# Two attention blocks on one core: MLP kept in rows, group norm per image, residual rows on GpSimd, one product of query and key weights

## The chip, the cores and the metric

One core of one Trainium2 chip. The metric is the device time of one execution in microseconds (us). Engine names: PE is TensorE (matrix products and transposes), DVE is VectorE, ACT is ScalarE, POOL is GpSimd, SP issues the DMAs. Each engine works through its own list of instructions in order; between engines the program waits on semaphores that are written out by hand.

## What is computed

The input x is 4 images of 16x16 pixels and 128 channels, all in float32. Layer 0 is a deformable attention with 8 heads, followed by an MLP; layer 1 is a group norm and a full attention inside each image. Cut to what the change touches:

```python
# layer 0, after q, the offsets and the 64 sampled keys of each image
attn = softmax(einsum(qh, kh)); msa = att @ mo_w + mo_b
z = msa + x
out0 = gelu(layernorm(z, ln_g, ln_b) @ mlp_w + mlp_b) + z
# layer 1, on v = out0
xg = group_norm(v, 32 groups of 4 channels over an image) * gn_gamma + gn_beta
q = (xg @ wq + bq) / sqrt(128); k = xg @ wk + bk; val = xg @ wv + bv
out = softmax(q @ k.T) @ val @ wo + bo + v
```

## The kernel before

The channels are 128, so one image is two tiles of 128 pixels (T = 8 tiles, B = 4 images). "Rows" means pixels on the partitions and channels along the free dimension; "transposed" means channels on the partitions and the 256 pixels of an image along it.

The program is one `build` function (line 69) in which each engine's list is written out: helper functions for each step, then a long sequence of calls. Nothing is scheduled by a compiler. The steps that matter here are these.

- Loads (lines 266 to 275) and normalisation of x, a convolution as 256 small products on PE, the offsets, the sampling weights `bilin` and the sampled keys. This fills the first 23 us.
- First attention, tile by tile (0 to 7): PE makes the scores of all heads (`score_tile`), DVE takes their maximum (`max_tile`, line 684) and subtracts it (`shift_tile`, line 691), PE transposes (`transpose_scores`, line 1099), ACT takes the exponential (`exp_tile`, line 451), PE multiplies with the values and with ones (`value_tile`), ACT inverts the sum by a logarithm and an exponential (lines 458, 465), DVE scales (`norm_tile`, line 700), PE projects (`out_project`), DVE adds the residual (`z_tile`, line 705). There is one set of four PSUM banks for the scores, so `score_tile(i)` waits for `shift_tile(i - 1)`.
- Norm of z and MLP, image by image: statistics on DVE, `z_scale` on POOL (a power of -0.5, line 334), `z_offset` on DVE (line 726), z_hat on ACT or DVE, two transposes (z and z_hat) on PE, the MLP in transposed form with `mlp_wg`, GELU on ACT, the sum `x1_t` on DVE (line 732). PE then transposes x1 back (`x1_transpose`, line 1168) and DVE adds the output bias to it (`x1_residual`, line 737): that is the residual in rows for the end.
- Group norm in two sets of two images: `gn_stats`, `gn_aggr` on DVE (lines 742, 746), `gn_apart` on PE (means of a group), `gn_square` and `gn_mean` on DVE (lines 752, 758), `gn_spread` on PE, `gn_var` on DVE (line 763), `gn_pow` on POOL (line 340), `norm_image` on DVE (line 769). The gamma is folded into three weights on POOL (`weights_scale`).
- Second attention, image by image: products q, k and v on PE (`project_q`, `project_k`, `project_v`), copied out by DVE (q, line 776) and ACT (k, line 495; v, line 489); scores (`score_image`), maximum on DVE (line 781), exponential on ACT (line 503), transposes of the probabilities p on PE (line 1250), copies (line 245), product with v, and `finish_tile` on DVE (lines 789, 791). SP sends y to memory.

A matmul of float32 stands as two records in the trace, a transpose as one. All matmuls but the transposes are recorded at the helper's line 917. The trace names a tensor without its digits, so `q1` is q, `k1` is k, `p1` is p and `v1` is v, and the PSUM banks 1 to 4 are called score.

## Time and profile before

| | us |
|---|---|
| median of 3 runs (lowest, highest) | 70.53 (70.19, 70.92) |
| the profiled execution, its own time | 71.08 |
| its span (first to last instruction) | 69.2 |
| PE busy in the span | 62.3 |
| DVE busy | 45.7 |
| ACT busy | 39.1 |
| POOL busy | 19.7 |

Times in the trace count from the start of the span. Neighbouring instructions of one engine overlap a little, since the next one is started before the last one has written out; so the distance of two starts (the pitch) is shorter than the duration of one, and both are used below. TensorE's granted clock was at its full 1.00 in every stretch.

### The profile page before, as it was taken

The numbers are of one execution on the slowest core, as the hardware profiler recorded it, in microseconds if no ns is written. First come the engines' busy times: TensorE is split into PE (matmuls) and PEld (weight loads), VectorE is DVE, ScalarE is ACT, GpSimd is POOL, SyncE is SP. The second block draws the span as 40 slices with busy tenths as digits, with TensorE's granted clock in tenths as the row PEclk, the third lists the DMA queues.
The fourth block names the chain that finished last, engine by engine and source line by source line (L and its number), as shares of the span: only waits on it lengthen the run. The fifth ranks groups of instructions, "written<-read, shape, count | busy, mean of one in ns | idle before, by whom it ended". The sixth has DMA issues, their size and how long they took to land.

```text
span 69.2 us, 2174 instructions
## 1 busy us (share of the span) xinstructions
PE 62.3 (90%) x822; PEld 47.5 (69%) x822; DVE 45.7 (66%) x154; ACT 39.1 (56%) x103; POOL 19.7 (28%) x31
## 2 busy tenths in 40 slices
PE   4999789988999998999979899998999999999940
PEld 1326379977587746786769778665578889998930
DVE  0258973102724598856999988699599894677570
ACT  5210349821920497758454799996272399849400
POOL 6002999994000001938004231321300300000000
PEclk9999999999999999999999999999999999999999
DMA  0779794000000000000000000000000000020212
GB/s 0 190 219 244 205 387 164 9 0 0 9 0 9 0 0 0 5 9 0 0 0 5 9 0 0 0 0 0 0 9 0 0 0 0 0 76 5 76 66 86
DMA packets 3051, 3.08 MB, mean 45 GB/s; under 512 B 225, under 2 KB 2657, under 8 KB 3042
## 3 DMA queue, kind: packets, MB, share of 16 engines
q1 hardware_dynamic: 3042, 2.96, 14.0%
q8 instruction: 6, 0.10, 0.6%
q14 instruction: 3, 0.02, 0.1%
HBM read 2.44 MB, written 0.52 MB: 43 GB/s over the span
## 4 chain that ended last, share of the span: by engine, by line
PE 57%; DVE 18%; issue 7%; DMA 6%; ACT 5%; SPq 2%; DVEq 0%; ACTq 0%
PE bank L917 30%; PE score L917 21%; DMA x_hw<-x 6%; DVE smax L684 4%; DVE s_sub L691 2%; PE bank L1099 2%; ACT p_t L451 2%; ACT log_sum L458 1%; DVE y L791 1%; SPq L267 1%; PE bank L1250 1%; PE score L1250 1%; DVE st L612 1%; DVE zst L709 1%; DVE q_conv L601 1%
## 5 line engine op out<-in xcount | busy, mean ns | idle before, releaser
L684 DVE TENSOR_REDUCE smax<-score 128x8 f32<-128x512 f32 x8 | 5.5, 690 | 1.6 <-PE score L917 1.4
L917 PE MATMUL bank<-q_ph,wd 128*32 128x84 f32 (+5 forms) x256 | 6.2, 249 | 0.0
L917 PEld LDWEIGHTS bank<-q_ph,wd 128*32 128x32 f32 x256 | 5.4, 110 | 1.1 <-ACT q_ph L382 0.8
L917 PE MATMUL score<-warm 128*128 128x512 bf16 x12 | 5.0, 569 | 1.0 <-POOL warm L289 1.0
L691 DVE TENSOR_TENSOR s_sub<-score,smax 128x512 f32<-128x512 f32 x8 | 5.5, 690 | 0.2
L318 POOL TENSOR_TENSOR x_res<-x_st,msa_bias 128x1024 f32<-128x1024 f32 x1 | 2.4, 2369 | 11.0 <-ACT msa_bias L423 11.0
L300 POOL TENSOR_TENSOR wd<-pack_early 128x512 f32<-128x512 f32 x4 | 4.1, 1046 | 4.9 <-DVE x_hat L624 4.9
L917 PE MATMUL score<-k_blk,qh 32*128 32x128 f32 x64 | 4.0, 319 | 1.2 <-DVE s_sub L691 1.1
L451 ACT ACTIVATE p_t<-bank 128x512 f32<-128x512 f32 x8 | 4.5, 592 | 0.9 <-PE bank L1099 0.9
L1099 PE MATMUL bank<-pack_early,s_sub 128*128 128x128 f32 x32 | 5.0, 285 | 0.0
L334 POOL TENSOR_TENSOR zrs<-zve,neg_half 128x2 f32<-128x2 f32 x4 | 2.8, 697 | 7.2 <-DVE zve L717 7.2
L917 PEld LDWEIGHTS score<-k_blk,qh 32*128 32x128 f32 x64 | 2.6, 182 | 2.9 <-issue 2.7
L612 DVE BATCH_NORM_STATS2 st<-x_hw 128x6 f32<-128x128 f32 x8 | 1.8, 283 | 3.7 <-DMA x_hw<-x 3.7
L503 ACT ACTIVATE p<-bank,nmax 128x256 f32<-128x256 f32 x8 | 3.5, 475 | 1.1 <-DVE nmax L781 1.0
L1099 PEld LDWEIGHTS bank<-pack_early,s_sub 128*128 128x128 f32 x32 | 3.4, 141 | 1.1 <-issue 0.4
L917 PE MATMUL bank<-k,q 128*128 128x256 f32 x16 | 3.9, 384 | 0.0
L634 DVE COPY q_ph<-score 128x256 f32<-128x256 f32 x2 | 0.8, 425 | 4.4 <-PE score L917 4.4
L917 PE MATMUL score<-q_conv,pack_early 128*32 128x128 f32 x64 | 2.5, 275 | 1.1 <-DVE q_conv L601 0.6
L917 PEld LDWEIGHTS score<-warm 128*128 128x128 bf16 x12 | 1.4, 130 | 3.1 <-issue 2.1
L495 ACT ACTIVATE k<-score,cols 128x256 f32<-128x256 f32 x4 | 1.9, 474 | 2.6 <-DVE q L776 2.6
L917 PE MATMUL bank<-p_t,v_blk 128*32 128x128 f32 x64 | 3.3, 280 | 0.0
L340 POOL TENSOR_TENSOR grs<-gve,neg_half 128x2 f32<-128x2 f32 x2 | 1.4, 690 | 6.7 <-DVE gve L763 6.7
(180 smaller groups left out, 161.6 us busy)
## 6 DMA issues: line engine op xcount, KB each, us to landing
x_st<-x SPq DMA_DIRECT2D x1, 512.0 KB, 6.8
pack_late<-late SPq DMA_DIRECT2D x1, 448.0 KB, 7.4
out<-y SPq DMA_DIRECT2D x3, 128.0 KB, 1.7
pack_fold<-fold SPq DMA_DIRECT2D x1, 320.0 KB, 4.7
pack_mid<-mid SPq DMA_DIRECT2D x1, 273.0 KB, 5.8
x_hw<-x SPq DMA_DIRECT2D x2, 128.0 KB, 2.4
x_hw<-x SPq DMA_DIRECT2D x1, 256.0 KB, 4.2
pack_early<-early SPq DMA_DIRECT2D x1, 184.0 KB, 2.7
```

What stands on the lines that cost most here:

```text
L300: pool.tensor_tensor(wd[:, n:n + WD_CHUNK].rearrange("p n k j -> p (n k) j"), w("ident32").unsqueeze(1).to_broadcast([P, WD_CHUNK * PHASES ...
L318: pool.tensor_tensor(x_res[:, :, :], x_st[:, :, :].rearrange("p b (s c) -> p (b s) c", s=S), msa_bias[:, :].unsqueeze(1).to_broadcast([P, ...
L334: pool.tensor_tensor(zrs[:, 2 * b:2 * b + 2], zve[:, 2 * b:2 * b + 2], neg_half[:, 0:2], ALU.pow).then_inc(s["zrs_ok"], 1)
L340: pool.tensor_tensor(grs[:, i], gve[:, i], neg_half[:, i], ALU.pow).then_inc(s["grs_ok"], 1)
L451: act.activation(p_t[:, i % 2].rearrange("p j q -> p (j q)"), tile_bank(i)[:, :], ACT.Exp).then_inc(s["exp_ok"], 1)
L495: act.activation(k1[:, b], bank[3 + b % 2][:, HW:2 * HW], ACT.Identity, bias=cols1[:, 1:2]).then_inc(s["k1_ok"], 1)
L503: act.activation(p1[:, b % 2, t], bank[5 + b % 2][:, t * HW:(t + 1) * HW], ACT.Exp, bias=nmax1[:, 2 * b + t:2 * b + t + 1]).then_inc(s["p1 ...
L612: dve.bn_stats(st[:, i], x_hw[:, i]).then_inc(s["stats"], 1)
L684: dve.tensor_reduce(smax[:, i % 2].rearrange("p (j e) -> p j e", e=2), scores, AX.X, ALU.max).then_inc(s["smax_ok"], 1)
L691: dve.tensor_tensor(s_sub[:, i % 2].rearrange("p (j e) q -> p j e q", e=2), scores, smax[:, i % 2].rearrange("p (j e) -> p j e", e=2).unsq ...
L917: return pe.matmul(o, l, r_, start=start, stop=stop, **k)
L1099: m = pe.transpose(tile_bank(i)[:, j * P:(j + 1) * P], s_sub[:, i % 2, 2 * j:2 * j + 2].rearrange("p h q -> p (h q)"), w("ident"))
```

## The change

Numerically the same function is computed, in another form:

- **MLP in rows.** z is transposed (not z_hat), into columns 256 to 511 of the image's own PSUM bank (`image_bank`, banks 1 to 4), and stays there. Mean subtraction is folded into the weights once (`centre_weights`: centre matrix times `mlp_wg`), and 1/std is applied to each row after the product, by DVE (`mlp_rows`, 8 instructions), with a bias row made of ln_b and mlp_b. GELU then gives rows. PE transposes these and adds them onto the z columns in PSUM (`x1_add`), so x1 transposed is never copied: group statistics and `norm_image` read it from PSUM.
- **Residual rows on POOL.** z + out_bias (`residual_rows`, 4 instructions) and then + GELU rows (`x1_rows`, 4 instructions). DVE's `x1_image` and `x1_residual` and PE's `x1_transpose` are gone.
- **Group norm image by image.** Four sets of one image. Gamma and beta are applied by DVE with the scale (`gn_affine`: gscale and gshift), and `weights_scale` on POOL is gone.
- **One product of query and key weights.** a1 = wq1 wk1^T is made once, q1 is x_gn through a1, and the scores take x_gn itself in place of k. `project_k` and ACT's `key_image` are gone. The part of the scores that belongs to one query only would cancel in the softmax; it comes out of one more column of the v product, and is added to and taken from the maximum (`own_term` on ACT, `shift_image` on DVE).
- Biases come in by one more DMA (`biases`, 128 x 384) between the loads of mid and x_st; bias sums are made by DVE from PSUM in the first attention (`residual_bias_out`, `mlp_bias_out`, `out_bias_out`). `residual_of_x` on POOL also waits for the second half's `bilin`.
- The lists of all four engines are written in another order around all of this.

```diff
             def residual_of_x():
+                pool.wait_ge(s["bilin_ok"], G)
                 pool.wait_ge(s["msabias_ok"], 1)
...
-            def weights_scale():
...
+            def residual_rows(b):
+                pool.wait_ge(s["z_ok"], 2 * b + 2)
+                pool.wait_ge(s["outbias_ok"], 1)
+                pool.tensor_tensor(z_out[:, 2 * b:2 * b + 2], z[:, 2 * b:2 * b + 2], out_bias[:, :].unsqueeze(1).to_broadcast([P, S, C]),
+                                   ALU.add).then_inc(s["zout_ok"], 1)
+
+            def x1_rows(b):
+                pool.wait_ge(s["zout_ok"], b + 1)
+                pool.wait_ge(s["gel_ok"], b + 1)
+                pool.tensor_tensor(x1_res[:, 2 * b:2 * b + 2], z_out[:, 2 * b:2 * b + 2], gel[:, 2 * b:2 * b + 2], ALU.add).then_inc(s["x1res_ok"], 1)
...
+            def mlp_rows(i):
...
+                dve.scalar_tensor_tensor(out=mlp_in[:, i], in0=image_bank(i // S)[:, i % S * C:(i % S + 1) * C], scalar=zrs[:, i:i + 1],
+                                         in1=mlp_bias[:, :], op0=ALU.mult, op1=ALU.add).then_inc(s["mlpin_ok"], 1)
...
+            def gn_affine(n):
...
+                dve.tensor_scalar(gscale[:, i], grs[:, i], w("gn_gamma"), None, ALU.mult).then_inc(s["gscale_ok"], 1)
+                dve.wait_ge(s["gscale_ok"], n + 1)
+                for b in GN_SETS[n]:
+                    dve.scalar_tensor_tensor(out=gshift[:, b:b + 1], in0=gmean[:, b:b + 1], scalar=gscale[:, b:b + 1], in1=w("gn_beta"),
+                                             op0=ALU.mult, op1=ALU.subtract).then_inc(s["gshift_ok"], 1)
...
+            def shift_image(b):
...
+                for i in (2 * b, 2 * b + 1):
+                    dve.scalar_tensor_tensor(out=shift1[:, i:i + 1], in0=nmax1[:, i:i + 1], scalar=own1[:, i:i + 1], in1=own1[:, i:i + 1],
+                                             op0=ALU.subtract, op1=ALU.add).then_inc(s["shift1_ok"], 1)
...
+            def centre_weights():
+                pe.wait_ge(s["mlpw_ok"], 1)
+                pe.wait_ge(s["late_in"], 16)
+                pe.wait_ge(s["z_ok"], 1)
+                mm(bank[5][:, 0:C], w("centre"), mlp_wg[:, :]).then_inc(s["centre_mm"], 1)
 
             def fold_second():
                 pe.wait_ge(s["late_in"], 16)
-                pe.wait_ge(s["z_ok"], 1)
+                pe.wait_ge(s["mlpwc_ok"], 1)
                 mm(bank[5][:, 0:C], w("wv1T"), w("wo1"))
-                mm(bank[5][:, C:C + 1], w("wq1"), w("gn_beta"))
-                mm(bank[5][:, C + 1:C + 2], w("wk1"), w("gn_beta")).then_inc(s["fold1_mm"], 1)
+                mm(bank[5][:, C:C + 1], w("wq1T"), w("bk1"))
+                mm(bank[5][:, C + 1:C + 2], w("bq1").to_broadcast([P, P]), w("bk1"))
+                mm(bank[5][:, C + 2:C + 3], w("wk1T"), w("bq1"))
+                mm(bank[5][:, 2 * C:3 * C], w("wq1T"), w("wk1T"))
+                mm(bank[5][:, 3 * C:4 * C], w("bv1").to_broadcast([P, P]), w("wo1")).then_inc(s["fold1_mm"], 1)
...
-            def project_k(b):
-                project_ready(b)
-                mm(bank[3 + b % 2][:, HW:2 * HW], wk1g[:, :], x_gn[:, b]).then_inc(s["k1_mm"], 1)
...
+                mm(image_bank(b)[:, 0:HW], a1[:, :], x_gn[:, b]).then_inc(s["q1_mm"], 1)
...
-                    m = mm(bank[5 + b % 2][:, t * HW:(t + 1) * HW], q1[:, b, t * P:(t + 1) * P], k1[:, b])
+                    m = mm(score1_bank(b)[:, t * HW:(t + 1) * HW], q1[:, b, t * P:(t + 1) * P], x_gn[:, b])
```

How the lists moved, at the three places that the prediction speaks of. First POOL, from the residual of x to the end, before:

```order
20 L318 TENSOR_TENSOR x_res<-x_st,msa_bias 128x1024
21 L324 TENSOR_TENSOR k_blk<-k_t,pack_mid 128x2x128
22 L344 TENSOR_SCALAR wq1g<-pack_late,pack_early 128x128
23 L345 TENSOR_SCALAR wk1g<-pack_late,pack_early 128x128
24 L347 TENSOR_SCALAR w_vog<-w_vo,pack_early 128x128
25 L334 TENSOR_TENSOR zrs<-zve,neg_half 128x2 x4
26 L340 TENSOR_TENSOR grs<-gve,neg_half 128x2 x2
```

and POOL in the changed kernel (z_out is `residual_rows`, the later x_res are `x1_rows`, grs is `gn_pow`):

```order
20 L331 TENSOR_TENSOR x_res<-x_st,msa_bias 128x1024
21 L337 TENSOR_TENSOR k_blk<-k_t,pack_mid 128x2x128
22 L358 TENSOR_TENSOR z_out<-z,out_bias 128x256 x2
23 L347 TENSOR_TENSOR zrs<-zve,neg_half 128x2 x3
24 L358 TENSOR_TENSOR z_out<-z,out_bias 128x256 x2
25 L347 TENSOR_TENSOR zrs<-zve,neg_half 128x2
26 L353 TENSOR_TENSOR grs<-gve,neg_half 128x1
27 L364 TENSOR_TENSOR x_res<-z_out,gel 128x256
28 L353 TENSOR_TENSOR grs<-gve,neg_half 128x1
29 L364 TENSOR_TENSOR x_res<-z_out,gel 128x256 x3
30 L353 TENSOR_TENSOR grs<-gve,neg_half 128x1 x2
```

A row of 256 elements now stands right behind each of the first two powers of the group norm, and three of them stand ahead of the last two.

DVE from the first normalised image to the first maximum of the second attention, before:

```order
82 L769 TENSOR_SCALAR x_gn<-x_t,gmean,grs 128x256 x2
83 L732 TENSOR_TENSOR x_t<-gel_t,score 128x256
84 L732 TENSOR_TENSOR x_t<-gel_t,bank 128x256
85 L742 BN_STATS gst<-x_t 128x6 x2
86 L746 BN_AGGR gmv<-gst 128x2 x2
87 L776 TENSOR_SCALAR q<-score,cols 128x256
...
94 L769 TENSOR_SCALAR x_gn<-x_t,gmean,grs 128x256
95 L781 TENSOR_REDUCE nmax<-bank 128x2
```

and in the changed kernel:

```order
90 L792 TENSOR_SCALAR x_gn<-score,gscale,gshift 128x256
91 L777 TENSOR_SCALAR gve<-bank 128x1
92 L756 BN_STATS gst<-score 128x6 x2
93 L784 TENSOR_SCALAR gscale<-grs,pack_early 128x1
94 L787 SCALAR_TENSOR_TENSOR gshift<-gmean,gscale,pack_early 128x1
95 L760 BN_AGGR gmv<-gst 128x2 x2
96 L792 TENSOR_SCALAR x_gn<-score,gscale,gshift 128x256
...
106 L784 TENSOR_SCALAR gscale<-grs,pack_early 128x1
107 L787 SCALAR_TENSOR_TENSOR gshift<-gmean,gscale,pack_early 128x1
108 L792 TENSOR_SCALAR x_gn<-score,gscale,gshift 128x256
109 L803 TENSOR_REDUCE nmax<-bank 128x2
```

The first maximum (nmax) now stands behind the scale and shift of the last image (rows 106 and 107), and the statistics of images 2 and 3 behind the normalising of image 0.

PE from the scores of image 0 of the second attention to the end, before:

```order
119 L917 MATMUL bank<-k,q 128x256 x4
120 L917 MATMUL score<-x_gn,wk1g 128x256
121 L917 MATMUL score<-x_gn,wq1g 128x256
122 L1250 MATMUL score<-pack_early,p 128x128 x2
123 L917 MATMUL score<-x_gn,wk1g 128x256
124 L1250 MATMUL bank<-pack_early,p 128x128 x2
125 L917 MATMUL score<-x_gn,wq1g 128x256
126 L917 MATMUL bank<-v,p_t 128x129 x4
...
131 L917 MATMUL score<-w_vog,x_gn 128x128 x2
...
134 L917 MATMUL score<-w_vog,x_gn 128x128 x2
```

and in the changed kernel:

```order
120 L960 MATMUL bank<-x_gn,q 128x256 x4
121 L960 MATMUL bank<-w_vo,x_gn 128x129 x2
122 L960 MATMUL score<-x_gn,a 128x256 x2
123 L1249 MATMUL score<-pack_early,p 128x128 x4
124 L960 MATMUL bank<-x_gn,q 128x256 x2
125 L960 MATMUL bank<-v,p_t 128x130 x4
126 L1249 MATMUL score<-pack_early,p 128x128 x4
127 L960 MATMUL bank<-w_vo,x_gn 128x129 x2
```

All q products and all v products but the last stand ahead of the first transposes of p; before, k and q of image 3 and two v products stood behind them.

## Rows read from the trace of the kernel before

**Rows 1.** The page: chain that ended last, share of the span by engine.
```profile
PE 57%; DVE 18%; issue 7%; DMA 6%; ACT 5%; SPq 2%; DVEq 0%; ACTq 0%
```
**Rows 2.** One stretch: us, busy (count) of PE, PEld, DVE, ACT, POOL; clock, DMA.
```profile
50.76:59.33 8.57, 8.57 (x53) 7.45 (x53) 7.01 (x21) 5.68 (x13) 0.69 (x1) 1.00 0.00 0
```
**Rows 3.** Timeline, first attention, tiles 2 and 3: start us, us, engine, line, instruction.
```profile
27.07 0.41 DVE L664 SCALAR_TENSOR_TENSOR bilin<-hat_x,hat_y 128x256 f32<-128x256 f32 x1
27.29 0.50 PE L917 MATMUL score<-k_blk,qh 32*128 32x128 f32 x8 [0.30 <-DVE s_sub L691]
27.91 0.69 DVE L684 TENSOR_REDUCE smax<-score 128x8 f32<-128x512 f32 x1 [0.43 <-PE score L917]
29.48 0.50 PE L917 MATMUL score<-k_blk,qh 32*128 32x128 f32 x8 [0.21 <-DVE s_sub L691]
```
**Rows 4.** Timeline, first attention, ACT before tile 2, PE's fold, last s_sub.
```profile
26.24 0.42 ACT L399 ACTIVATE hat_y<-abs_y 128x256 f32<-128x256 f32 x1
35.46 0.51 PE L917 MATMUL bank<-pack_early,pack_late 128*128 128x1 f32 x4
39.86 0.69 DVE L691 TENSOR_TENSOR s_sub<-score,smax 128x512 f32<-128x512 f32 x1
```
**Rows 5.** Timeline, group norm of images 0 and 1.
```profile
46.83 0.74 DVE L742 BATCH_NORM_STATS2 gst<-x_t 128x6 f32<-128x256 f32 x2
48.27 0.35 DVE L752 SCALAR_TENSOR_TENSOR dev<-bank,gmv 128x1 f32<-128x1 f32 x2
49.49 0.69 POOL L340 TENSOR_TENSOR grs<-gve,neg_half 128x2 f32<-128x2 f32 x1 [2.59 <-DVE gve L763]
50.29 0.73 DVE L769 TENSOR_SCALAR x_gn<-x_t,gmean,grs 128x256 f32<-128x256 f32 x2 [0.88 <-POOL grs L340]
```
**Rows 6.** Groups by shape from 30 us on: busy, mean ns, idle before.
```profile
L776 DVE TENSOR_SCALAR q<-score,cols 128x256 f32<-128x256 f32 x4 | 1.9, 484 | 1.0 <-PE score L917 1.0
...
L791 DVE SCALAR_TENSOR_TENSOR y<-bank,rec,x_res 128x128 f32<-128x128 f32 x5 | 1.8, 350 | 0.2
L769 DVE TENSOR_SCALAR x_gn<-x_t,gmean,grs 128x256 f32<-128x256 f32 x4 | 1.6, 408 | 1.0 <-POOL grs L340 0.9
...
L324 POOL TENSOR_TENSOR k_blk<-k_t,pack_mid 128x256 f32<-128x256 f32 x1 | 0.6, 613 | 1.1 <-ACT k_t L443 1.1
...
L752 DVE SCALAR_TENSOR_TENSOR dev<-bank,gmv 128x1 f32<-128x1 f32 x4 | 0.7, 218 | 0.0
...
L726 DVE SCALAR_TENSOR_TENSOR z_shift<-zmv,zrs 128x2 f32<-128x2 f32 x3 | 0.5, 151 | 0.4 <-POOL zrs L334 0.4
```
**Rows 7.** Timeline, DVE and POOL beside each other, early and at 46 us.
```profile
8.55 1.04 POOL L300 TENSOR_TENSOR wd<-pack_early 128x512 f32<-128x512 f32 x1
8.89 0.72 DVE L629 SCALAR_TENSOR_TENSOR shift<-mv,rstd 128x4 f32<-128x4 f32 x1
46.22 0.69 POOL L334 TENSOR_TENSOR zrs<-zve,neg_half 128x2 f32<-128x2 f32 x1 [2.10 <-DVE zve L717]
46.49 0.42 DVE L732 TENSOR_TENSOR x_t<-gel_t,bank 128x256 f32<-128x256 f32 x1
```
**Rows 8.** Timeline, second attention to the first transposes of p.
```profile
55.45 0.69 DVE L781 TENSOR_REDUCE nmax<-bank 128x2 f32<-128x512 f32 x1
56.53 1.21 ACT L503 ACTIVATE p<-bank,nmax 128x256 f32<-128x256 f32 x3
57.12 0.38 PE L1250 MATMUL score<-pack_early,p 128*128 128x128 f32 x2
57.34 0.60 PE L917 MATMUL score<-x_gn,wk1g 128*128 128x256 f32 x2
57.78 0.38 PE L1250 MATMUL bank<-pack_early,p 128*128 128x128 f32 x2
```
**Rows 9.** Timeline, the end of the last product and the last output row.
```profile
64.96 1.50 PE L917 MATMUL score<-v,p_t 128*128 128x129 f32 x12
66.81 0.35 DVE L791 SCALAR_TENSOR_TENSOR y<-score,rec,x_res 128x128 f32<-128x128 f32 x1
```

More of the change, by code:

```diff
@@ L66, with build @@
 PLACE = {pack: columns(parts) for pack, parts in PACKS.items()}
-def build(nc, x, early, fold, mid, late, rows, ln_rows, out):
+def build(nc, x, early, fold, mid, late, rows, ln_rows, bias_rows, out):
     ctx = ExitStack()
@@ L212, in conv_views @@
             return src, dst
-        GN_SETS = [range(0, 2), range(2, 4)]
+        GN_SETS = [range(b, b + 1) for b in range(B)]
         def tile_bank(i):
@@ L356, in _ @@
             z_scale(2)
+            residual_rows(2)
+            residual_rows(3)
             z_scale(3)
             gn_pow(0)
+            x1_rows(0)
             gn_pow(1)
+            x1_rows(1)
+            x1_rows(2)
+            x1_rows(3)
+            gn_pow(2)
+            gn_pow(3)
         @block.scalar
@@ L465, in inverse_tile @@
                 act.activation(inv_sum[:, i % 2], log_sum[:, i % 2], ACT.Exp, scale=-1.0).then_inc(s["inv_ok"], 1)
-            def zhat_image(b):
-                act.wait_ge(s["zshift_ok"], b + 1)
-                for i in (2 * b, 2 * b + 1):
-                    act.activation(z_hat[:, i], z[:, i], ACT.Identity, scale=zrs[:, i:i + 1], bias=z_shift[:, i:i + 1]).then_inc(s["zhat_ok"], 1)
             def zt_image(b):
                 act.wait_ge(s["zr_mm"], b + 1)
-                act.wait_ge(s["zt_mm"], b + 1)
-                act.copy(z_t[:, 2 * b:2 * b + 2, :].rearrange("c s q -> c (s q)"), zt_bank(b)[:, 0:HW]).then_inc(s["zt_ok"], 1)
+                act.copy(z_t[:, 2 * b:2 * b + 2, :].rearrange("c s q -> c (s q)"), x1_cols(b)).then_inc(s["zt_ok"], 1)
@@ L1311, in _ @@
             values_half(1)
-            value_tile(0)
+            out_project(0)
             value_tile(1)
             transpose_scores(2)
+            centre_weights()
             score_tile(4)
             transpose_scores(3)
+            fold_second()
+            score_tile(5)
             value_tile(2)
-            out_project(0)
+            value_tile(3)
             out_project(1)
-            score_tile(5)
-            value_tile(3)
-            fold_second()
             score_tile(6)
@@ L1435 @@
     }
[L1436 removed]
+    for n in ("dw_b", "bq", "mq_b", "bv", "mk_b", "mv_b", "ln_g", "ln_b"):
         data[n] = col(get[L0 + n])
```

506 lines of the change are left out of this document (234 added, 272 removed).

## The prediction

> **What bounds the kernel now.** I read the chain of waits first: 57% of the span is PE, 18% DVE, 5% ACT [rows 1]. PE is the bound on average, but an average says nothing of a stage, so I went through the timeline stage by stage. In the first attention neither PE nor DVE is the bound alone: `score_tile` starts at 27.29 and 29.48, a period of 2.19, made of the scores (0.50), the maximum from 27.91 (0.69), the subtraction (0.69) and three hand-overs [rows 3]. That loop between two engines sets the stage; the last s_sub ends at 39.86 + 0.69 = 40.55 [rows 4]. Between 46.83 and 50.29 group norm is a chain of round trips, statistics to x_gn in 3.46 us [rows 5]. From 50.76 PE is busy 8.57 of 8.57 us [rows 2]: here it is the bound, until its last product ends at 64.96 + 1.50 = 66.46. The last y ends at 66.81 + 0.35 = 67.16, and the last DMA fills the rest of the span of 69.2 [rows 9].
>
> The change takes work from PE where PE is the bound, and gives more and smaller work to DVE ahead of that. I laid the new lists against the times of before, stage by stage.
>
> **Until the last s_sub: +0.4.** Up to tile 0 PE has the same products in another order, each still busy to the next: 0. The added DMA and the longer late pack are not waited for by anything near them, since POOL reaches `mlp_weights` late: 0. Then two places touch the loop.
> - Tile 2. ACT now has `exp_tile(0)` ahead of the second `abs_half` and `hats_half`. Before, hat_y starts at 26.24 [rows 4] and `bilin` at 27.07 [rows 3]. The exponential waits for the transposes, which end at about 26.15, and takes 0.6; then |y| and the hat, 0.42 each: hat_y is done at 27.6, `bilin` (0.41 long, pitch 0.33) and `mlp_bias_out` (0.2) stand ahead of the maximum, which starts at 28.15, not 27.91: +0.24.
> - Tiles 4 and 5. `centre_weights` stands ahead of score 4 and `fold_second` ahead of score 5. Two products of one column take 0.51 [rows 4], about 0.21 each in pitch; six of them and the transposes before them end some 0.15 to 0.2 after the loop would want PE. The three bias sums and z tiles on DVE (0.2 each) fall in the gaps in which DVE waits for scores, or cost 0.1 where they stand between maximum and subtraction.
> Sum +0.4 (bounds: 0, if all fits in the gaps; +1.1, all three bias sums and 0.5 of the products in full).
>
> **From there to the first x_gn: about -0.6, so -0.2 in total before the next item.** z_hat, its two transposes per image and ACT's share of them are gone, but `z_transpose` waits for the last s_sub, and the last two `out_project` stand behind the MLP products of images 0 and 1. By pitches z(7) is done near 45.7 against 45.13. The chain doesn't go through it, though: it goes inverse, table load, GELU 0, `x1_add` 0, statistics at 46.7 against 46.83 [rows 5]. From there one image instead of two takes 0.37 + 0.17 of statistics, two round trips to PE (0.35 each), square, variance (0.16 to 0.2), the power 0.69 plus hand-overs, then two more instructions, gscale and gshift, 0.17 each, and some 0.7 of `mlp_rows` between them: x_gn starts at 50.1 against 50.29.
>
> **Forms that before does not show.** `mlp_rows` is taken as y is, 0.35 long [rows 6] and 0.27 in pitch. x_gn now reads PSUM: between 0.408 (its own row, from SBUF) and 0.484 (q, same size, from PSUM) [rows 6]; I take the latter, +0.08 each. `x1_add` is a transpose that adds onto PSUM: as a plain one two of them hold PE for 0.22 (p at 57.12 to the next at 57.34 [rows 8]), as a product of the same size for 0.44; if the latter, +0.2 on the way to each image's statistics, at most 0.4 at the end; below the plain one it can't go, as it moves the same columns. I take the plain one. Statistics from PSUM: between 0 and the same 0.08.
>
> **Two collisions of POOL and DVE: +0.4.** The trace has a row that bears on this. DVE's shift, 128x4 from two tensors in SBUF, takes 0.72 us where z_shift, the same operation on 128x2, takes 0.151 [rows 6, 7]. It starts at 8.89, while POOL runs a wd instruction of 1.04 from 8.55, and ends at 9.61, just as that one ends (9.59) [rows 7]. At 46.49 DVE's x_t, with one input in SBUF and one in PSUM, runs beside POOL's power and keeps its 0.42 [rows 7]. So an instruction with both inputs in SBUF waits for POOL's. In the changed kernel that is gshift (gmean and gn_beta), and POOL's list has `x1_rows(0)` right behind `gn_pow(0)`, and `x1_rows(1)` right behind `gn_pow(1)`. Such a row takes 0.61 (k_blk, the same size) [rows 6]. gshift would end 0.46 after the power; with the row in front of it, at 0.61 + 0.06 = 0.67: 0.21 each, 0.42 for both. Bounds: 0, and twice 0.6 if the start falls badly. I take 0.42. For images 2 and 3 POOL has no more than the other power behind, and gshift 3 comes after it: 0.
>
> The Trainium skill, "SBUF — State Buffer", section on the two separate sides, says that VectorE and GpSimd share one pair of ports as an exclusive lock, and that an instruction of VectorE with two SBUF inputs or in a 2-port mode takes part in it. The first half agrees with the 0.72 us. By its second half gscale (one SBUF source) could be held too; that would change little, since gshift behind it waits for the same end.
>
> **From the first projection to the first transposes of p: +0.5.** Before, the products for v0, q0, k0, k1, q1, v1, the scores of images 0 and 1 and k2, q2 run here without a gap, and p is transposed at 57.12 [rows 8]. Now the k's are gone, but DVE's list holds the next thing back: the statistics of images 2 and 3 stand behind `norm_image(0)`, their scale and shift (with two powers in a row on POOL, 0.69 each) stand ahead of `max_image(0)`. By pitches: gmv of image 3 at 51.9, gve at 53.5, the powers until 54.95, gshift 3 at 55.3, x_gn 2 until 55.7, maximum 55.73 against 55.45 [rows 8], then two more small ones (`shift_image`), exponential at 56.6 against 56.53, and both tiles of p are needed: transposes at 57.6. PE idles some 1.7 us in this stretch, which is all that the four products of k (0.44 each by the pitch of wk1g at 57.34 to the transposes at 57.78 [rows 8]) would have given.
>
> **From the first transposes of p to the last product: -1.14.** This is 57.12 to 66.46 before, 9.34 us. Behind the first transposes stood k3, q3, v2, v3: now only v3 does. Three products at 0.44 are 1.3 less. Against that, gaps of some 0.16, since the second exponential of image 3 and its copy now come close to the last products. So 8.2.
>
> The end moves by +0.48 - 1.14 = -0.66 without the collisions, -0.24 with them. 71.08 of the profiled execution becomes 70.84; it lies 0.55 over the median of the runs (70.53), so I forecast 70.3 us.
>
> **Rivals.**
> - PE stays the bound and every product that went counts: four k's at 0.44 are 1.76, the end moves by -1.7, 68.8 us. For it: 8.57 of 8.57 busy [rows 2]. Against it: DVE's list, as above. It holds if the maximum of image 0 starts before 55.
> - Group norm image by image pays: the statistics of 2 and 3 do not hold the maximum, and there are no gaps from the first transposes: only the -1.14 counts, 69.4 us. For it: x1 3 is in PSUM at about 50, so that 3 us are there for it. Against: the list order.
> - Slower: DVE becomes the bound of the group norm. Between 46 and 56 its list now has 20 instructions of one column (square, mean, variance, scale, shift, four each) and 8 `mlp_rows`. I counted the small ones by pitch: two squares together last 0.35 where one lasts 0.218 [rows 5, 6], so the second starts 0.13 after the first. If each stands alone behind a semaphore, it costs its duration, some 0.2, which is 0.07 more: 1.4 us for 20, and the end moves by +1.2: 71.7 us. It decides from the point where no two of them stand back to back; the pairs of images 2 and 3 speak against it, the eight round trips to PE and POOL for it. DVE's load speaks for it too: by my pitches it has 11.3 us of work in the 12.2 us ahead of the first maximum.
> - That the change would not do what it says can't be here: the products of k are out of PE's list.
>
> **How the numbers follow.** Forecast (70.3) 0.40, with an own range of 69.7 to 71.1; PE-bound (68.8) 0.20; group norm pays (69.4) 0.15; slower by DVE (71.7) 0.25. Within 1% of 70.53, about what a measurement of this kernel can tell from no change, is 69.82 to 71.24. Faster takes the 0.35 of both fast cases and 0.05 from the forecast's lower edge: 0.40. Slower takes 0.25, and as much of its lower edge falls inside 1% as of the forecast's upper edge outside: 0.25. Same 0.35. The range for 8 in 10 goes from 68.7 to 71.6: it takes in both fast cases and the slow case's nearer half.
>
> **What would show it.** Right: last s_sub near 41.0; first gshift over 0.3 us long beside a POOL row; first nmax of the second attention after 55.5 with DVE busy or waiting for grs before it; PE with over 1 us idle between the first projection and the first transposes of p; last product near 66. Wrong: PE without gaps from 50 on (first rival), gshift at 0.17 (no collision), or s_sub 7 later than 41.5 (the loop bears more than I gave it).

## The result: slower, 74.3 us, and the profile after

| | before | after |
|---|---|---|
| median (lowest, highest) | 70.47 us (70.19, 70.92), 4 runs | 74.34 us (72.44, 75.60), 4 runs |
| ratio, runs at full clock | | 1.033, interval 1.020 to 1.046 |
| profiled execution, its own time | 71.08 | 75.60 |
| its span | 69.2 | 72.7 |
| time outside the span | 1.9 | 2.9 |

The forecast was 70.3 us with 71.6 as the upper end. The runs of the changed kernel spread far more than those of before; the two short ones (72.44, 73.22) had a granted clock of 1.00 on average, the two long ones 0.95. So the miss has two parts: even the short runs lie 2.4 us over the kernel before and outside the range, with the clock at 1.00, and the long ones, of which the profiled one is one, lose some 2.7 us more.

The page of after, the rows that matter (the clock row is in 40 slices of 1.8 us):

```profile
span 72.7 us, 2191 instructions
PE 64.1 (88%) x822; PEld 49.5 (68%) x822; DVE 47.6 (66%) x172; ACT 35.8 (49%) x96; POOL 24.4 (34%) x38
...
PEclk9999999999999999999999999999975559999999
...
PE 67%; DVE 19%; issue 5%; ACT 4%; POOL 1%; DVEq 0%; ACTq 0%; POOLq 0%
```

PE's share of the chain rose from 57% [rows 1] to 67%, although its list lost four products of 256 columns. The clock row says why: a stretch of 5s near the end. The windows of the same profile around it (us, busy time and count of PE, PEld, DVE, ACT, POOL; granted clock; DMA share; GB/s):

```profile
49.00:51.60 2.60, 1.81 (x12) 1.25 (x11) 2.29 (x11) 0.83 (x2) 1.23 (x2) 1.00 0.03 6
51.60:53.50 1.90, 1.55 (x10) 1.15 (x10) 1.79 (x8) 0.37 (x1) 1.84 (x3) 1.00 0.00 0
53.50:56.30 2.80, 2.80 (x13) 2.62 (x13) 1.86 (x11) 0.00 (x0) 1.79 (x4) 0.51 0.00 0
56.30:59.70 3.40, 3.40 (x10) 2.68 (x10) 2.42 (x8) 2.34 (x5) 0.03 (x1) 0.50 0.01 2
```

PE was idle for 0.79 of 2.60 us and 0.35 of 1.90 us at full clock, and then the granted clock fell to 0.5, which is 1.2 GHz in place of 2.4, for 6.7 us. Where rows 2 had 8.57 of 8.57 us at 1.00, "busy" now means the same products at half the rate. The timeline of after at the places that the prediction named:

```profile
40.98 0.69 DVE L704 TENSOR_TENSOR s_sub<-score,smax 128x512 f32<-128x512 f32 x1
...
50.19 0.72 POOL L364 TENSOR_TENSOR x_res<-z_out,gel 128x256 f32<-128x256 f32 x1
50.34 0.21 DVE L784 TENSOR_SCALAR gscale<-grs,pack_early 128x1 f32<-128x1 f32 x1 [0.24 <-POOL grs L353]
...
50.58 0.35 DVE L787 SCALAR_TENSOR_TENSOR gshift<-gmean,gscale,pack_early 128x1 f32<-128x1 f32 x1
50.97 0.54 DVE L792 TENSOR_SCALAR x_gn<-score,gscale,gshift 128x256 f32<-128x256 f32 x1
...
51.57 0.71 PE L960 MATMUL bank<-w_vo,x_gn 128*128 128x129 f32 x4 [0.72 <-DVE x_gn L792]
...
56.28 3.62 PE L960 MATMUL bank<-x_gn,q 128*128 128x256 f32 x8
...
58.23 0.69 DVE L803 TENSOR_REDUCE nmax<-bank 128x2 f32<-128x512 f32 x1 [0.87 <-PE bank L960]
...
61.33 0.60 PE L1249 MATMUL score<-pack_early,p 128*128 128x128 f32 x4
...
67.54 0.63 PE L1249 MATMUL score<-pack_early,p 128*128 128x128 f32 x4 [0.72 <-DVE p_t L252]
...
70.38 0.35 DVE L821 SCALAR_TENSOR_TENSOR y<-bank,rec,x_res 128x128 f32<-128x128 f32 x1
```

The scores of images 0 and 1 take 3.62 us. From such starts the whole difference of the two profiled executions can be laid out, from one landmark to the next:

| stretch | before | after | difference |
|---|---|---|---|
| to the first smax | 23.48 | 24.00 | +0.5 |
| to the last s_sub (rows 4) | 16.38 | 16.98 | +0.6 |
| to the first x_gn (rows 5) | 10.43 | 9.99 | -0.4 |
| to the first transposes of p (rows 8) | 6.83 | 10.36 | +3.5 |
| to the last y (rows 9) | 9.69 | 9.05 | -0.6 |
| start of the last y to the end of the time | 4.27 | 5.22 | +0.9 |

The last row reaches outside the span: the measured time less the start of the last y. The sum is +4.5, 75.60 less 71.08. Two entries make nearly all of it. Of the 3.5 the prediction had 0.9 (its own times for the two ends are 7.7 us apart); for the rest, and for the tail, it had no price.

### The profile page after: what moved, and what is told of

It reads as the page before. It is cut to its first block, busy times and chain, and to the rows that moved or that the text cites. A ratio compares the mean times of both kernels' runs of the same rounds, so it can differ in the third digit from the quotient of the medians.

```text
span 72.7 us, 2191 instructions
## 1 busy us (share of the span) xinstructions
PE 64.1 (88%) x822; PEld 49.5 (68%) x822; DVE 47.6 (66%) x172; ACT 35.8 (49%) x96; POOL 24.4 (34%) x38
## 4 chain that ended last, share of the span: by engine, by line
PE 67%; DVE 19%; issue 5%; ACT 4%; POOL 1%; DVEq 0%; ACTq 0%; POOLq 0%
PE bank L960 40%; PE score L960 21%; PE bank L1150 5%; PE score L1249 2%; DVE gst L756 2%; DVE s_sub L704 2%; DVE smax L697 2%; DVE mlp_in L751 2%; DVE y L821 1%; DVE q_conv L614 1%; DVE rec L819 1%; ACT inv_sum L489 1%; DVE gshift L787 1%; DVE nmax L803 1%; ACT p_t L475 1%
## 5 line engine op out<-in xcount | busy, mean ns | idle before, releaser
L960 PE MATMUL bank<-x_gn,q 128*128 128x256 f32 x16 | 5.7, 506 | 0.0
L358 POOL TENSOR_TENSOR z_out<-z,out_bias 128x256 f32<-128x256 f32 x4 | 2.9, 728 | 7.5 <-DVE z L718 7.5
L506 ACT COPY v<-bank 128x258 f32<-128x258 f32 x4 | 1.5, 374 | 6.2 <-PE bank L960 6.2
L960 PEld LDWEIGHTS bank<-x_gn,q 128*128 128x128 f32 x16 | 3.9, 263 | 0.6
L519 ACT ACTIVATE p<-bank,shift 128x256 f32<-128x256 f32 x8 | 3.5, 475 | 1.4 <-DVE shift L811 1.4
L960 PE MATMUL bank<-w_vo,x_gn 128*128 128x129 f32 x16 | 3.5, 353 | 0.7 <-DVE x_gn L792 0.7
L960 PEld LDWEIGHTS bank<-w_vo,x_gn 128*128 128x128 f32 x16 | 3.1, 261 | 1.1 <-DVE x_gn L792 1.0
L803 DVE TENSOR_REDUCE nmax<-bank 128x2 f32<-128x512 f32 x4 | 2.7, 685 | 1.5 <-PE bank L960 1.5
```

The costliest lines, as they stand in the source:

```text
L358: pool.tensor_tensor(z_out[:, 2 * b:2 * b + 2], z[:, 2 * b:2 * b + 2], out_bias[:, :].unsqueeze(1).to_broadcast([P, S, C]), ALU.add).then_ ...
L519: act.activation(p1[:, b % 2, t], score1_bank(b)[:, t * HW:(t + 1) * HW], ACT.Exp, bias=shift1[:, 2 * b + t:2 * b + t + 1]).then_inc(s["p1 ...
L803: dve.tensor_reduce(nmax1[:, t], score1_bank(b)[:, :].rearrange("p (t m) -> p t m", t=2), AX.X, ALU.max, negate=True).then_inc(s["nmax1_ok ...
L960: return pe.matmul(o, l, r_, start=start, stop=stop, **k)
```

## The experiments

Each kernel below ran on the same chip beside runs of the kernel before, and its ratio is to these. "Outside" is the time of a run less its span.

### First group: the clock, the collision, the ninth input

The changed kernel again, unchanged (`again`):

> The changed kernel once more, unchanged. In its profile TensorE's granted clock is 0.5 from 53.5 to 59.7 us, right after a stretch (49 to 53.5) in which PE is busy only 3.4 of 4.5 us. Theory clock gate: the clock is lost in some executions and kept in others, so the times fall in two groups some 2.5 to 3 us apart, the lower one near 72.8. Theory noise: one group. Either way the time outside the span should be about 3.0 us, against 1.9 for the kernel before.

74.06 us median of 6, before 70.77. The times do not fall in two groups; they spread from 71.83 to 75.59. The granted clock of the six runs goes with their spans: 1.00 has 68.8, 0.973 has 69.8, 0.967 has 71.4, 0.95 has 71.8 to 72.4. Outside the span they have either 2.1 to 2.2 or 3.0 to 3.6 us, where before has 1.9 to 2.3. In the profiled one the clock was low for a shorter time (0.73 and 0.58 in the windows 51.6 to 56.3), 3.2 us in place of 6.7.

Warm products in the gaps (`warm_gaps`):

```diff
             gn_apart(1)
+            keep_warm(1, at=0)
             x1_add(2)
...
             x1_add(3)
+            keep_warm(3, at=0)
             project_v(0)
             project_q(0)
+            keep_warm(2, at=0)
             gn_apart(2)
```

> The changed kernel with six products of the warm tile (bf16, 512 columns, about 0.22 us each) put into PE's gaps between the group norm products of image 1 and those of image 2; nothing reads them. Theory clock gate: the clock stays at 1.00 in every execution, all times between 72.2 and 73.4. Theory that the clock falls for another reason (the number of transposes, the phase of the chip): still two groups, and each 0.2 us later.

72.89 us, ratio 1.032 (1.028 to 1.036). Its windows and its scores:

```profile
49.00:51.60 2.60, 2.52 (x16) 1.65 (x16) 2.22 (x10) 0.54 (x2) 1.86 (x4) 1.00 0.00 0
51.60:53.50 1.90, 1.90 (x13) 1.32 (x11) 1.87 (x10) 0.25 (x1) 1.83 (x3) 1.00 0.03 9
53.50:56.30 2.80, 2.80 (x18) 2.32 (x18) 2.49 (x10) 1.85 (x3) 1.06 (x2) 1.00 0.00 0
...
54.15 1.89 PE L960 MATMUL bank<-x_gn,q 128*128 128x256 f32 x8
```

Work that does nothing makes the median 1.2 us shorter (74.06 to 72.89): the clock stays (0.99 to 1.00 in all six runs), and the scores take 1.89 in place of 3.62 us. First x_gn to the first transposes of p is 7.80 us here, 8.86 in `again`, 10.36 in the profile of after. So the fall of the clock is a cause, and it costs 1 to 2.6 us in the executions in which it happens. It is not all: without warm products the two runs of after that kept the clock have a ratio of 1.033, and the only one of `again` has 71.83 us. So the warm products gain nothing beyond the clock, and some 2 us over the kernel before have another reason. Counted over all runs, the clock was under 0.98 in 11 of 16 without warm products (after, `again`, `no_collision`) and in 1 of 55 with them (here and in the variants below).

The two collisions taken away (`no_collision`: `x1_rows(0)` waits for the first x_gn, the others for what follows):

> The changed kernel with POOL's residual rows held back until the image's x_gn is written, and those of images 2 and 3 behind the last powers. Theory collision: gshift of images 0 and 1 takes 0.2 instead of 0.35 us, x_gn 0 and 1 start 0.15 and 0.3 us earlier, executions at full clock gain 0.3 us, and a shorter PE gap may keep the clock more often. Rival: gshift keeps its 0.35, as it comes from being the first behind a wait, and nothing moves.

```profile
49.71 0.22 DVE L790 SCALAR_TENSOR_TENSOR gshift<-gmean,gscale,pack_early 128x1 f32<-128x1 f32 x1
49.97 0.54 DVE L795 TENSOR_SCALAR x_gn<-score,gscale,gshift 128x256 f32<-128x256 f32 x1
50.59 0.73 POOL L364 TENSOR_TENSOR x_res<-z_out,gel 128x256 f32<-128x256 f32 x1 [1.23 <-DVE x_gn L795]
```

gshift takes 0.22 where it took 0.35 beside POOL's row, and x_gn starts 0.26 behind it in place of 0.39: the collision exists and costs 0.13 us (the second one 0.15). The time gained nothing (74.58, and ratio 1.032 from the two of six runs that kept the clock), since POOL's row now holds the second power back: gscale waits 0.69 us for it at 51.94, and first x_gn to the first transposes of p is 8.48 us.

This profile is one of the two that kept the clock, and PE has two gaps in it that are together longer than those of after:

```profile
50.56 0.71 PE L963 MATMUL bank<-w_vo,x_gn 128*128 128x129 f32 x4 [0.59 <-DVE x_gn L795]
...
52.55 0.61 PE L963 MATMUL bank<-gmv,pack_late 128*128 128x1 f32 x4 [0.84 <-DVE gmv L763]
...
54.48 1.89 PE L963 MATMUL bank<-x_gn,q 128*128 128x256 f32 x8
```

In the 4.5 us up to 53.0 PE is idle for 1.51 us, and the scores still take 1.89; in after and `again` it was idle for 1.14 and 1.15 of the 4.5 us before the fall. So idle time of this kind can bring the clock down and need not: what decides it in one execution no run here shows.

The ninth input alone, on the kernel before (`extra_input`: one more DMA of 192 KB that nothing reads):

> The kernel before with one more input tensor and its DMA (128 x 384, broadcast from 3 rows), which nothing reads. Theory that the time outside the span (3.0 us after, 1.9 before) comes with the ninth input: 71.5 us, with the span as before, about 69.2. Rival, that it belongs to something else or to the day: 70.5 us, and outside the span 1.9.

Ratio 0.996 (0.993 to 0.998), outside 2.0. The additional load costs nothing that the medians show; in its one profile the time from the end of the last y to the end is 4.10 us, against 3.92 in before.

### Second group: what lies behind the last instruction, and what the keys are worth

> The changed kernel with the six warm products of the run warm_gaps, and 24 further products of one column at the start, where PE waits for the first load. A queue row shows one instruction load of 16 KB behind the end of the span in the kernel before (0.8 to 1.3 us behind it) and in the changed kernel (2.2 to 2.9 us behind it), and the time ends with it. In warm_gaps, with 12 more PE instructions, that load falls at 66 to 67, and the last two output DMAs are issued 0.9 us late. Theory of the late load: about 50 more PE instructions bring the load to 62 to 65, where nothing waits for it: the output DMAs are issued without delay and the median is 71.4 to 71.9. Rival, the extra microsecond belongs to something else (the number of DVE instructions, the last semaphores): the median stays at 72.6 to 73.2 and span plus outside time as in warm_gaps.

> The kernel before with the same 24 products of one column at the start. Theory of the late load: the load moves from behind the span to 60 to 65 and the time falls, by up to 1 us (69.8 to 70.5 against 70.77); if the outside time of before is what every program has, nothing changes (ratio 0.997 to 1.003). Rival, more instructions cost time by themselves: 71 or more.

> The kernel before with 18 small memsets more on DVE at the start, where DVE waits for x; the changed kernel has 18 DVE instructions more than before. Theory of the late load on PE: no change, ratio 0.997 to 1.003, outside time 2.0. Rival, DVE's number of instructions is what the end waits for: outside time about 3, ratio 1.013 to 1.018.

Windows that reach beyond the span show a last load of 16 KB (the page lists its queue as instructions). In `again`, whose span ends at 69.8, 2.2 to 2.4 us behind it:

```profile
71.80:72.00 0.20, 0.00 (x0) 0.00 (x0) 0.00 (x0) 0.00 (x0) 0.00 (x0) 0.50 0.00 0
72.00:72.20 0.20, 0.00 (x0) 0.00 (x0) 0.00 (x0) 0.00 (x0) 0.00 (x0) 0.50 0.35 82
```

and in before, whose span is 69.2, 0.8 to 1.0 us behind it:

```profile
70.00:70.20 0.20, 0.00 (x0) 0.00 (x0) 0.00 (x0) 0.00 (x0) 0.00 (x0) 1.00 0.30 82
```

In `warm_gaps` it came at 66.8 to 67.0, just as the first of the last two output DMAs was issued, and that issue took 1.31 us where others take 0.35. Its row, and that of before, where two together take 0.84:

```profile
66.89 1.31 SPq L295 DMA_DIRECT2D out<-y  x1
```

```profile
66.73 0.84 SPq L283 DMA_DIRECT2D out<-y  x2
```

`warm_pad` missed the time it was to have: 73.30 us, where before had 70.94; its two shortest runs give the ratio 1.021 (1.012 to 1.031). The outside time is 2.2 to 2.3 in all seven runs, so the long tails are gone, but PE stood still in the convolution, for nothing that the profile names (`issue`):

```profile
16.05 0.36 PE L960 MATMUL bank<-q_ph,wd 128*32 128x98 f32 x4 [1.40 <-issue]
...
21.11 0.72 PE L960 MATMUL bank<-q_ph,wd 128*32 128x112 f32 x19 [0.80 <-issue]
```

It looks like a wait for instructions, but that isn't shown: the loads of 16 KB near it land at 13.8 and 18.9, 0.9 and 1.4 us before the two stalls begin. `before_pad`: 0.999 (0.994 to 1.003), outside 1.8, no such stall. `before_dvepad`: 1.002 (0.998 to 1.007), outside 1.9 to 2.2: the number of DVE instructions is not the cause of the longer tail.

The keys alone (`no_keys`):

```diff
-            project_k(0)
-            project_k(1)
...
-                    m = mm(bank[5 + b % 2][:, t * HW:(t + 1) * HW], q1[:, b, t * P:(t + 1) * P], k1[:, b])
+                    m = mm(bank[5 + b % 2][:, t * HW:(t + 1) * HW], q1[:, b, t * P:(t + 1) * P], x_gn[:, b])
```

> The kernel before without the four products of k and their copies: the scores take x_gn in place of k, so the key weights and bias are left out. It prices what the change could have taken from PE if nothing else had moved. If PE is the bound and its clock stays: -1.8 us (ratio 0.975). If the gaps that open (x_gn 1, the maxima and exponentials come no earlier) take back a part: -0.6 to -1.2. If PE then idles enough for its clock to fall: the windows of 51 to 60 show a granted clock under 1.00 in the slow runs, and the time is anywhere from -1 to +2.

Ratio 0.992 (0.987 to 0.997): -0.6 us, not -1.8. A gap opens at once:

```profile
52.11 0.38 PE L912 MATMUL bank<-gmv,pack_late 128*128 128x2 f32 x2 [0.57 <-DVE gmv L742]
```

A stretch in which PE is 100% busy is not one in which every product counts: DVE stands close behind, and two thirds of what leaves PE becomes idle time.

### Third group: narrow warm products, and another order

`warm_narrow` has 5, 16 and 11 products of 96 columns where `warm_gaps` had 1, 3 and 2 of 512.

> The changed kernel with 32 warm products of 96 columns in the same three gaps, in place of the 6 of 512 columns of warm_gaps: about the same columns, 52 more PE instructions than in warm_gaps, and none of them at the start. In warm_gaps the last instruction load of PE fell 0.4 us after the first of the last two output DMAs was issued (that issue took 1.31 us), in warm_pad 0.6 us before (0.59 us, and PE also stood 1.40 and 0.80 us in the convolution, waiting for instructions). Theory of the late load: it now falls at 60 to 64, the last two issues take 0.35 to 0.38 each, the outside time is 2.1 to 2.3 in every run, and the median is 71.7 to 72.2. Rival, the tail is longer for another reason: 72.6 to 73.1, with span plus outside time as in warm_gaps. Clock 1.00 in both.

72.24 us, ratio 1.019 (1.011 to 1.027), outside 2.1 to 2.2 in all six runs, the two last issues together 0.84. The load comes at 63.6. From the end of the last y to the end of the time are 4.17 us, where `again` had 5.15, `warm_gaps` 5.11 and before 3.92. So 0.9 us went with the place of the load (the two kernels differ in nothing else than the shape and number of the warm products). In `warm_pad` the load lands at 67.7 to 67.8, 1.3 us ahead of the issue at 69.09 and not 0.6, and that issue still took 0.59: nearness in time is not the whole account. With `hat_first` below this is the fastest version with the change in it, and still 1.9% slower than before.

> warm_narrow with ACT's order of before at one place: the second |y| and hat ahead of exp_tile(0). The prediction gave the other order +0.24 us. Theory: the hat is ready 0.5 to 0.6 earlier, the maximum of tile 2 starts 0.2 earlier, and the last s_sub and the end come 0.15 to 0.25 earlier than in warm_narrow (by the profiles, from the first smax on). Rival, PE's list (products of the folds) sets the loop: last s_sub at the same distance of 16.97 from the first smax, same time.

1.018 (1.011 to 1.025), the same. The maximum of tile 2 starts at 28.53 in both profiles, but this one had its first maximum 0.28 us earlier (23.56 against 23.84): counted from there it is 0.28 later, and the last s_sub 0.29 later (17.26 against 16.97). The hat is early, and DVE waits 0.51 us for the scores in its place. They stand behind `value_tile(0)`, which now waits 0.24 us for the exponential that the hat pushed back.

> warm_narrow with another order in the second attention: ACT copies q of images 0 and 1 (DVE did) and loads the exponential's table ahead of v0, DVE takes the maximum of image 0 ahead of the scales of images 2 and 3, PE makes the scores of image 0 ahead of gn_spread(2), and of image 3 ahead of v3, and the copy of p of (2, 1) stands ahead of finish_tile(1, 0). Theory (what holds the end is that image 0's maximum stands behind the small instructions of images 2 and 3 on DVE): first nmax 1.5 to 2 us earlier than in warm_narrow, transposes of p from about 56.3 instead of 57.9, last product 1.0 to 1.6 earlier, median 70.3 to 71.1. Rival A, DVE is full either way: x_gn of images 2 and 3 come later by what image 0 gains, and the end moves by less than 0.4. Rival B, the gaps that open on PE bring the clock down again: granted clock under 1.00 between 54 and 60, 72 to 75.

73.45 us, 1.035 (1.028 to 1.042): nearest to rival A, but the end moved by 2.0 us where it said under 0.4, and DVE is not full, it waits 0.69 us for PE and 0.67 for POOL. Rows of the profile:

```profile
54.45 0.69 DVE L811 TENSOR_REDUCE nmax<-bank 128x2 f32<-128x512 f32 x1 [0.69 <-PE bank L966]
...
55.67 1.06 POOL L353 TENSOR_TENSOR grs<-gve,neg_half 128x1 f32<-128x1 f32 x2 [1.63 <-DVE gve L784]
...
58.78 0.54 DVE L799 TENSOR_SCALAR x_gn<-score,gscale,gshift 128x256 f32<-128x256 f32 x1
```

Image 0's maximum is 2.0 us earlier than in `warm_narrow` (56.50) and x_gn of image 3 is 1.3 us later (57.48 there). The end follows the latter; the other 0.7 us may be the wait that scores 3 ahead of v3 bring, seen in `q_on_act` below.

### Fourth group: what was still open

> warm_narrow, and in the first attention: z_tile(0) behind shift_tile(3) on DVE, centre_weights behind score_tile(4) and fold_second behind score_tile(5) on PE, the hat ahead of exp_tile(0) on ACT. Theory (these places cost the loop its 0.6 us): first smax to last s_sub 16.4 to 16.6 in place of 16.97, the end 0.3 to 0.5 earlier than warm_narrow, ratio to before 1.012 to 1.015. Rival, the loop's gain is lost again ahead of the group norm (z(7), powers on POOL): last s_sub earlier, end within 0.1.

1.032 (1.028 to 1.036), slower by my own edit: first smax to last s_sub is 18.71 us. From tile 2 to tile 5 the maxima go from 27.98 to 34.78, 6.80 us, where `warm_narrow` needs 7.20 and before 6.86: `z_tile(0)` between a maximum and its subtraction, `centre_weights` and `fold_second` cost that 0.4. But `fold_second` later makes ACT's `fold_out` later, which stands ahead of `exp_tile(3)`, and the next maximum starts 4.04 us after the last:

```profile
34.78 0.69 DVE L697 TENSOR_REDUCE smax<-score 128x8 f32<-128x512 f32 x1 [0.57 <-PE score L960]
...
36.23 0.27 ACT L453 COPY w_vo<-bank 128x128 f32<-128x128 f32 x1 [2.37 <-PE bank L960]
...
38.82 0.68 DVE L697 TENSOR_REDUCE smax<-score 128x8 f32<-128x512 f32 x1
```

> warm_narrow, with q of images 0 and 1 copied by ACT and the exponential's table loaded ahead of v0, and on DVE x_gn of images 2 and 3 both ahead of the maximum of image 0; scores 0 ahead of v1, scores 3 ahead of v3, the copy of p (2, 1) ahead of finish_tile(1, 0). new_order gained 2 us on image 0's maximum and lost 1.9 us at the end. Theory (the end follows x_gn of image 3): x_gn 3 starts 0.9 to 1.2 earlier than in warm_narrow, image 0's maximum 0.2 to 0.5 later, the last product 0.5 to 1.0 earlier, ratio 1.005 to 1.012. Rival, image 0's chain holds PE now: transposes of p later, PE idle before them, end 0 to 0.5 later than warm_narrow.

1.023 (1.018 to 1.027). x_gn 3 starts at 56.64 (0.84 earlier than in `warm_narrow`), image 0's maximum at 57.10 (0.60 later), the last y at 68.91 in place of 67.66: later, as the rival said, but by image 0's chain for the smaller part only: first x_gn to the transposes is 8.12 against 7.80, +0.3. From there to the last y it is 9.95 against 9.05, +0.9, as in `q_on_act` below, which has the same wait of my own. So this run does not say what the order alone is worth.

> Both edits of loop_free and images_first. If they add up: 0.8 to 1.5 us under warm_narrow, ratio to before 0.998 to 1.008. If only one stage at a time holds the end: the better of the two alone.

1.055 (1.050 to 1.061), 75.01 us. The edits do add up, but as losses: from the first smax to the last y are 46.76 us against 43.82 in `warm_narrow`, +2.9, where `loop_free` alone has +1.9 and `images_first` alone +1.2.

> The kernel before with 6 products of one column more at the start (12 PE instructions, as many as warm_gaps added to the changed kernel). With 24 of them (before_pad) the last instruction load of PE went from behind the span to 6.5 us ahead of the last output packet, and the outside time from 1.9 to 1.8. Theory of the late load: now it falls 2 to 4 us ahead of the last output packet, among the issues of the last output DMAs; one of these takes 0.5 to 1.3 us in place of 0.35, and the time rises by 0.4 to 1.0 us (ratio 1.005 to 1.014). Rival, the load matters only in the changed kernel: ratio 0.997 to 1.003, issues of 0.35 to 0.38.

1.004 (1.001 to 1.007). Fine windows show the load still behind the span, by 0.7 to 0.9 us: the question was not put. (The 1.7 us of the next text count from the start of the last output packet, not from the end of the span.)

> The kernel before with 14 products of one column more at the start. With 6 the last instruction load stayed 1.7 us behind the span, with 24 it came 6.5 us ahead of the last output packet. Theory of the late load: with 14 it falls between, at 0 to 4 us ahead of the last output packet, one issue of an output DMA takes 0.5 to 1.3 us, and the time rises by 0.3 to 0.9 us (ratio 1.004 to 1.013). Rival, it costs nothing in this kernel wherever it falls: ratio 0.997 to 1.003. If the load stays behind the span or jumps ahead as with 24, the question stays open.

1.001 (0.996 to 1.006). The load falls at 63.6 to 63.8, 4.5 us ahead of the end of the span and 1.6 us ahead of the next issue of an output DMA (65.38); the last issues take 0.84 together, the outside time is 1.8. In the kernel before the load costs 0.1 us at most in the places where it fell, and it never fell on an issue.

> warm_narrow with DVE's order kept, but q of images 0 and 1 copied by ACT (0.48 us each off DVE), the exponential's table loaded ahead of v0, scores 0 ahead of v1, scores 3 ahead of v3, the copy of p (2, 1) ahead of finish_tile(1, 0). Theory (DVE's work in the group norm and its order as written hold the end): first nmax 0.3 to 0.6 earlier, last product 0.3 to 0.6 earlier, ratio 1.010 to 1.015. Rival, the round trips to POOL and PE hold it: DVE waits longer for grs instead, x_gn 2 at the same time, ratio 1.017 to 1.022.

1.028 (1.021 to 1.035). From the first x_gn to the first maximum are 5.70 us, as in `warm_narrow` (5.69): DVE, with two copies less, waits 0.41 us for PE and 0.51 for POOL instead. That is the rival's wait, though the time is above both ranges. And scores 3 ahead of v3 was a mistake; the stretch from the first transposes of p to the last y is 9.90 us in place of 9.05, with this wait in it:

```profile
63.28 0.35 DVE L819 SCALAR_TENSOR_TENSOR shift<-nmax,own 128x1 f32<-128x1 f32 x2 [0.79 <-ACT own L515]
```

The own term of an image comes out of its v product, so in this form v stands on the way to the exponential. Before, it did not.

## Why the prediction was wrong, point by point

- **"PE idles some 1.7 us in this stretch, which is all that the four products of k would have given."** This is the step that failed. There was such idle time: 1.34 us from the first projection to the first transposes of p in `no_collision`, whose clock stayed at 1.00. In after it was 0.35 there and 0.72 just ahead of the first projection, and then the products at half rate filled the rest. It was priced as time lost once. Rows 2 stood at clock 1.00 with PE never idle; what PE does after idle time was a cost that no row of before showed, and it should have had a bound and a rival. It measured 1.1 us (`again`) to 2.6 us (profile of after) between x_gn and the transposes, 1.2 us in the medians, and nothing in the runs that kept the clock, which miss by the next point and by the gaps further down. The Trainium skill, "TensorE: Matmul & The Clock Gate", section on HAM oscillation, tells that idle time between bursts of matmuls brings the clock down and that the products after it then run at half rate; the trace of after agrees, with 3.62 us against 1.89 for the same eight records, though the waits of the page's case are longer than any gap in it (0.72 us), and that of `no_collision` shows gaps without a fall. That page was there to be read ahead of the forecast.
- **The end: "-0.24".** This is the second step that failed, and it holds with the clock kept too: the prediction took the time outside the span as given, 1.9 us, a term put at nothing. It became 2.9. From the end of the last y to the end of the time are 4.9 to 5.2 us in the three profiles without warm products, and 4.2 where PE's last instruction load is moved away from the end (`warm_narrow` and the six variants of it). Of the rest of the tail, 4.2 against 3.8 to 3.9 us, no run found the cause; the ninth input may be part of it, by the 4.10 of `extra_input`. Nor is it shown why the load comes 0.8 us behind the span in before and 2.2 in the changed kernel, and whether it is the load itself that delays the end or something that comes with its place. The Trainium skill, "Runtime: NRT & Kernel Launch", section on instruction fetch, calls the cost of crossing such a block mostly hidden. In the middle of the program no row here speaks against it, since the stalls of `warm_pad` (1.40 and 0.80 us) begin after the loads have landed; whether it holds at the end of this kernel hangs on that open point.
- **Last s_sub +0.4.** Measured +0.6, within its bounds of 0 to 1.1 (the last s_sub ends at 41.67, past the 41.5 named as a sign, but 0.5 of that lies ahead of the first smax). Tile 2's maximum comes 2.51 us behind tile 1's (26.18 to 28.69) in place of 2.25: +0.26 for a forecast of 0.24, right in size, but `hat_first` shows that the hat alone is not the reason: with the hat ahead of the exponential the scores come later and the maximum with them, by 0.28. `z_tile` between maximum and subtraction was mis-sized: 0.2 for 0.1.
- **From s_sub to x_gn -0.6, and the collisions +0.42.** Only the first collision lies in this stretch, so -0.4 was forecast; -0.44 was measured, and -0.56 without the collision (`no_collision`). The collision is real, by the mechanism read from rows 7: gshift ends at 50.93, as POOL's row ends (50.91). It costs 0.13 and 0.15, not 0.21 each. The end was forecast well, 0.67 behind the power and 0.70 measured; what was mis-sized is the end without the row, 0.58 behind the power (`no_collision`) and not 0.46. By the second half of the Trainium skill's rule gscale could be held too: it takes 0.21 us beside POOL's row at 50.19 and 0.21 without one (`no_collision`), so it was not held; whether it ran in a 2-port mode no run shows. x_gn from PSUM takes 0.54, outside the bounds of 0.408 to 0.484 that I gave. POOL's rows take 0.72, not 0.61.
- **First transposes of p +0.48.** With the clock held (`warm_gaps`) the stretch from x_gn is 7.80 against 6.83, +0.97. The prediction's own times for it, x_gn at 50.1 + 0.21 and transposes at 57.6 + 0.42, are 7.7 apart: the order of the lists was read rightly, and `new_order` and `q_on_act` show what it rests on, the round trips to POOL and PE for images 2 and 3, rather than DVE's load.
- **From there to the last product -1.14.** Measured -0.64 to the last y. This is a mis-sized term: the gaps were put at 0.16; one alone is 0.72 (67.54, behind DVE's copy of p). `no_keys` says the same of the kernel before: its stretch from the transposes to the last y is 9.82 us against 9.69, though k3 was gone from PE.
- **The rivals.** The slower one had 0.25 and the wrong mechanism: small DVE instructions that stand alone. `q_on_act` speaks against DVE's load: with two copies less on DVE the first maximum comes no earlier. No rival had the clock or the tail, and these two were most of the miss: 70.84 forecast for the profiled execution, plus 2.6 for the clock, 0.9 for the tail, 0.5 for the start and 0.7 for terms mis-sized, is 75.5. With the clock kept the same terms give the profile of `warm_gaps`: 70.84, plus 1.2 for the tail and 0.7 for the terms, less 0.3 for the start, is 72.4, and 72.44 was measured.

Open: the 0.35 us of tail that no placement removes, what decides in one execution whether the clock falls, and the 0.5 us to the first smax, which differs from run to run in both kernels (22.6 in `again`, 24.00 in after; 22.59 in `before_pad14`, 23.96 in `before_pad6`); an issue gap of PE at 19 to 20 us (0.21 and 0.76 in the first two) is part of it.

## What to carry over

Before you take work from an engine that a trace shows 100% busy, ask who stands right behind it: here -1.8 us of products was worth 0.6. Whatever idle time a change opens on PE is to be priced twice, once as time and once as the clock that may be lost after it, and the products behind it are to be read at half rate for a rival; a few dummy products in the gaps, over several executions, tell which it was. And compare time less span of both kernels first: a microsecond there belongs to no row of the timeline.

## What the runs showed of the hardware that was not expected

- 0.8 us of idle PE within 2.6 us, and 0.35 within the next 1.9, were followed by a granted clock of 0.5 for 6.7 us, though no gap was longer than 0.72 us (after). In an execution of `no_collision` 1.51 us of idle time within 4.5 were not followed by a fall. With 32 products of 96 columns or 6 of 512 in the same gaps the clock stayed at 0.99 to 1.00 (`warm_narrow`, `warm_gaps`).
- Where a load of instructions (16 KB) met the issue of an output DMA, that issue took 1.31 us in place of 0.35 (`warm_gaps`); where it came behind the last DMA of the changed kernel, the time ended 0.7 to 1.0 us later than where it came 6 us ahead (4.87 to 5.15 us behind the last y against 4.17). In the kernel before its place made 0.1 us. That the load itself is the cause is not shown.
- With 24 one-column products more at the start (48 instructions) PE stood still for 1.40 and 0.80 us in the convolution of the changed kernel (`warm_pad`), waiting for nothing that the profile names, and not at all in the kernel before (`before_pad`).
- An instruction of DVE on two SBUF inputs beside a row of POOL ends as that row ends, and not a duration of its own later: gshift takes 0.35 us, 50.58 to 50.93, beside a row that ends at 50.91, and 0.22 alone (`no_collision`).
